# Linear attention on one core: the sine part of the rotated keys written by one VectorE operation instead of two

## The chip, the cores and the metric

One core of one Trainium2 chip runs the program. The metric is the device time of one execution in microseconds. It is given as the median of several runs of the same kernel. The profile is one further execution of it, taken by the hardware profiler.

## What is computed

The program is a chain of layers over x of shape (16, 256, 128): a convolution block, four linear attention layers, a feed-forward layer, and then attention and mixture-of-experts layers. The change lies in the linear attention. Cut to that:

```python
def rope(x):
    ...
    xp = x.reshape(b, n, half, 2)
    xr = jnp.stack([-xp[..., 1], xp[..., 0]], axis=-1).reshape(b, n, c)
    return x * cos + xr * sin

def linear_attention(x, Wq, bq, Wk, bk, Wv, bv, g, bb):
    q = gelu(x @ Wq + bq) + 0.21
    k = gelu(x @ Wk + bk) + 0.21
    v = x @ Wv + bv
    q_r, k_r = rope(q), rope(k)          # then all are split into 16 heads of 8
    z = 1.0 / (jnp.einsum('bhnd,bhmd->bhnm', q, kmean) + 1e-06)
    kv = jnp.einsum('bhnd,bhne->bhde', k_r, v) / n
    out = jnp.einsum('bhnd,bhde->bhne', q_r, kv) * z
    return layernorm(out + x, g, bb)
```

So the channels come in pairs. The rotated key is k*cos plus a sine part, in which each channel takes its partner's value with a sign.

## The kernel before

The program runs its layers as phases. A phase is a block of instruction streams, one for each engine, and a barrier stands between two phases. `linear_phase` holds the four linear attention layers. It works on one batch row of 256 tokens and one layer at a time, and there are 16 x 4 = 64 such units, numbered i. Four rows (U = 4) are in flight, and each has its own buffers and two PSUM banks, A and D. Unit i+4 is the next layer of the same row as unit i (or the first layer of a new row), and it needs what unit i has put out.

The order of work is written out by hand for each engine, in a loop over i from 0 to 66, and semaphores join the engines. In iteration i each engine works on several units:

- **TensorE (PE):** the projections of unit i (L555 for keys and values, L558 for queries); for unit i-1 the sum of the keys (L565), a transpose of the layer's input (L81), and the product of keys and values (L574); for unit i-2 the output (L600, L601); for unit i-3 the transposes back of the normalized rows (L81); then for unit i-1 the turned blocks (L581, which needs L515) and the divisors (L589).
- **VectorE (DVE):** for unit i-3 the statistics of the layer norm (L475, then L482); the bias of keys and values of unit i (L489, which takes what L555 left in PSUM); the reciprocal of unit i-2 (L494); `turn_k` of unit i (L499 for the cosine part into kc, L503 for the sine part into ks); the masked blocks of unit i-1 (L515, reads PSUM and the mask); `join_k` of unit i (L510, adds ks to kc); and the output of unit i-2 (L522, L527).
- **ScalarE (ACT):** gelu of the queries (L634) and of the keys (L639) of unit i; the normalization of unit i-3 (L650); the mean of the keys (L663, L666); the scaled output of unit i-3 (L657), which PE's L555 of unit i+1 needs; then small copies (L644, L671, L676).
- **GpSimd (POOL):** for unit i-3 the reciprocal root and the shift of the layer norm (L448, L449, L451, L454), after L482 and ahead of L650; then for unit i-1 the cosine and sine parts of the queries (L459, L460), each a product of two 256-element tiles in SBUF.

An iteration as it is spoken of here begins with L499 on DVE, so L515, L510, L522, L475, L482, L489 and L494 follow it. `turn_k` waits for gelu of the keys, writes kc in one instruction and ks in two: the first of these fills the even channels from the odd ones, the second the odd from the even. The sine table `sinT` carries the sign. All these tiles are float32 with 128 partitions, and 256 elements on each, 2 halves of 128 channels. No semaphore stands between the three instructions.

Of the kernel before, what the change touches and what calls it, by code (L numbers as in the profile page):

```python
# [12 lines left out]
ALU = mybir.AluOpType  # L13
# [18 lines left out]
GELU_SHIFT = 0.21  # L32
# [19 lines left out]
def semaphores(nc, ctx, prefix, names):  # L52

    sems = {n: nc.alloc_semaphore(f"{prefix}_{n}") for n in names.split()}

    def clear():
        nc.clear_and_free_semaphores(list(sems.values()))
        nc.all_engine_barrier()

    ctx.callback(clear)  # L60
    return sems
# [22 lines left out]
def spread(ap, n):  # L84

    return ap.unsqueeze(len(ap.shape)).broadcast_to([*ap.shape, n])
# [297 lines left out]
def linear_phase(nc, g):  # L384
# [3 lines left out]
    with ExitStack() as ctx:  # L388
        s = semaphores(nc, ctx, "la", "zero pkv pq kv q k qs ks kcs ksum kmean km kvm kvbd kv2 kv2s den dens z qc qsn out yz y "
                                      "stats mv ve nm rstd shift un unt h")  # L390

        def sb(name, shape, dt=F32):
            return ctx.enter_context(nc.sbuf_tensor("la_" + name, shape, dt))
# [5 lines left out]
        h = sb("h", [P, U, N])  # L399
        q = sb("q", [P, U, N])  # L400
        kv = sb("kv", [P, U, NT, 2 * C])
        k = sb("k", [P, U, NT, C])
        kc = sb("kc", [P, U, NT, C])
        ks = sb("ks", [P, U, NT, C])
# [20 lines left out]
        def layer(i):  # L425
            return i // U % L
# [10 lines left out]
        @block.gpsimd  # L437
        def _(pool):
            pool.memset(half[:, :], -0.5).then_inc(s["zero"], 1)
            pool.memset(eps[:, :], LN_EPS_A).then_inc(s["zero"], 1)  # L440
            pool.memset(minus[:, :], -1.0).then_inc(s["zero"], 1)
            pool.memset(ones[:, :], 1.0).then_inc(s["zero"], 1)
            pool.wait_ge(s["zero"], 4)

            def root(i):
                u = i % U
                pool.wait_ge(s["mv"], i + 1)
                pool.tensor_tensor(ve[:, u, :], mv[:, u, :, 1], eps[:, :], ALU.add).then_inc(s["ve"], 1)  # L448
                pool.tensor_tensor(nm[:, u, :], mv[:, u, :, 0], minus[:, :], ALU.mult).then_inc(s["nm"], 1)  # L449
                pool.wait_ge(s["ve"], i + 1)  # L450
                pool.tensor_tensor(rstd[:, u, :], ve[:, u, :], half[:, :], ALU.pow).then_inc(s["rstd"], 1)  # L451
                pool.wait_ge(s["nm"], i + 1)
                pool.wait_ge(s["rstd"], i + 1)
                pool.tensor_tensor(shift[:, u, :], nm[:, u, :], rstd[:, u, :], ALU.mult).then_inc(s["shift"], 1)  # L454

            def turn_q(i):
                u = i % U
                pool.wait_ge(s["qs"], i + 1)
                pool.tensor_tensor(qc[:, u, :], q[:, u, :], g["cosF"][:, :], ALU.mult).then_inc(s["qc"], 1)  # L459
                pool.tensor_tensor(qs[:, u, :], q[:, u, :], g["sinF"][:, :], ALU.mult).then_inc(s["qsn"], 1)  # L460

            for i in range(K + 3):
                if 0 <= i - 3 < K:
                    root(i - 3)
                if 0 <= i - 1 < K:
                    turn_q(i - 1)

        @block.vector
        def _(v):

            def stats(i):
                u = i % U
                v.wait_ge(s["y"], i + 1)
                for t in range(NT):
                    last = v.bn_stats(st[:, u, t, :], y[:, u, t, :])  # L475
                last.then_inc(s["stats"], 1)

            def aggr(i):
                u = i % U
                v.wait_ge(s["stats"], i + 1)  # L480
                for t in range(NT):
                    last = v.bn_aggr(mv[:, u, t, :], st[:, u, t, :])  # L482
                last.then_inc(s["mv"], 1)

            def take_kv(i):
                u = i % U
                bias = g["bkv"][:, layer(i), :].unsqueeze(1).broadcast_to([P, NT, 2 * C])
                v.wait_ge(s["pkv"], i + 1)
                v.tensor_tensor(kv[:, u], A[u].rearrange("p (h c) -> p h c", h=NT), bias, ALU.add).then_inc(s["kv"], 1)  # L489

            def inverse(i):
                u = i % U
                v.wait_ge(s["dens"], i + 1)
                v.reciprocal(z[:, u, :], z[:, u, :]).then_inc(s["z"], 1)  # L494

            def turn_k(i):
                u = i % U
                v.wait_ge(s["k"], i + 1)
                v.scalar_tensor_tensor(out=kc[:, u], in0=k[:, u], scalar=GELU_SHIFT, in1=g["cosT"][:, :, :],  # L499
                                       op0=ALU.add, op1=ALU.mult)  # L500
                for par in range(2):
                    a = [t.rearrange("p h (c t) -> p h c t", t=2) for t in (ks[:, u], k[:, u], g["sinT"][:, :, :])]
                    last = v.scalar_tensor_tensor(out=a[0][:, :, :, par], in0=a[1][:, :, :, 1 - par], scalar=GELU_SHIFT,  # L503
                                                  in1=a[2][:, :, :, par], op0=ALU.add, op1=ALU.mult)
                last.then_inc(s["ks"], 1)

            def join_k(i):
                u = i % U
                v.wait_ge(s["ks"], i + 1)
                v.tensor_tensor(kc[:, u], kc[:, u], ks[:, u], ALU.add).then_inc(s["kcs"], 1)  # L510

            def blocks(i):
                u = i % U
                v.wait_ge(s["kvm"], i + 1)
                v.scalar_tensor_tensor(out=kvbd[:, u, :], in0=A[u][:, 0:C], scalar=1.0 / N, in1=g["head_mask"][:, :],  # L515
                                       op0=ALU.mult, op1=ALU.mult).then_inc(s["kvbd"], 1)

            def scaled(i):
                u = i % U
                v.wait_ge(s["out"], i + 1)  # L520
                v.wait_ge(s["z"], i + 1)
                v.tensor_tensor(y[:, u].rearrange("p h (n d) -> p (h n) d", d=HD),  # L522
                                A[u][:, 0:N].rearrange("p (n d) -> p n d", d=HD),
                                spread(z[:, u, :], HD), ALU.mult).then_inc(s["yz"], 1)
                v.wait_ge(s["yz"], i + 1)
                yu = y[:, u].rearrange("p h c -> p (h c)")
                v.tensor_tensor(yu, D[u][:, 0:N], yu, ALU.add).then_inc(s["y"], 1)  # L527

            for i in range(K + 3):
                if 0 <= i - 3 < K:  # L530
                    stats(i - 3)
                if 0 <= i - 3 < K:
                    aggr(i - 3)
                if 0 <= i - 0 < K:
                    take_kv(i - 0)
                if 0 <= i - 2 < K:
                    inverse(i - 2)
                if 0 <= i - 0 < K:
                    turn_k(i - 0)
                if 0 <= i - 1 < K:  # L540
                    blocks(i - 1)
                if 0 <= i - 0 < K:
                    join_k(i - 0)
                if 0 <= i - 2 < K:
                    scaled(i - 2)
# [2292 lines left out]
```

## Time and profile before

| | us |
|---|---|
| runs of the kernel, median of 3 | 2293.94 |
| lowest and highest of them | 2292.66, 2307.22 |
| span of the profiled execution | 2374.1 |

The profiled execution is slower than the runs, so its durations are read for proportions and order, and a difference in time is set against the span first. In the rows below, times are microseconds from the start of the span unless they are marked ns. PE is TensorE's multiplication, PEld its weight loads, which overlap it. A row names the line of the kernel, the engine, what is written and what is read ("la_ks<-la_k,k_sinT"), the shapes (partitions x elements) and a count. Where neighbouring instructions of one line stand in one row (x2), the time is from the first one's start to the last one's end. "Idle before" and its arrow name what ended the engine's idle time. Instructions of an engine are pipelined, so that one can start slightly before the record of the one ahead ends.

### The profile page before, as it was taken

How to read it: one execution, taken by the hardware profiler on the slowest of the kernel's cores; microseconds unless marked ns; L12 is line 12 of the kernel's file. 1: busy time of each engine (PE TensorE's matmuls, PEld its weight loads, DVE VectorE, ACT ScalarE, POOL GpSimd, SP SyncE). 2: the span in 40 equal slices, each digit the busy share in tenths (PEclk: the TensorE clock that was granted, in tenths of full speed). 3: DMA queues.
4: the chain of work that ended last, by engine and by line, in shares of the span. 5: the costliest groups of instructions: out<-in, count | busy, mean ns of one | idle time of the engine just before them, and what ended most of it. 6: DMA issues, size and time to landing. Idle time of an engine off the chain costs nothing. (4 is left out here: it accounts for less than half of the span.)

```text
span 2374.1 us, 43139 instructions
## 1 busy us (share of the span) xinstructions
PE 1915.4 (81%) x14694; PEld 1329.8 (56%) x14694; DVE 1428.9 (60%) x4140; ACT 1180.8 (50%) x2785; POOL 1135.4 (48%) x2002
## 2 busy tenths in 40 slices
PE   7978999978776888786899888889488887678891
PEld 6866888866332343343455447778234443267781
DVE  6997999955663555475788844323478886333232
ACT  3435666653443677553566544334156764443340
POOL 2534555543354555345567672522666545124225
PEclk9998999999796999898899969899568977589995
DMA  8000000000000000000000005556000000045572
GB/s 259 1 1 1 1 1 1 2 1 0 1 1 1 1 2 1 1 1 1 2 2 2 10 29 154 157 176 194 18 20 6 2 1 24 14 129 176 169 205 78
DMA packets 93945, 109.50 MB, mean 46 GB/s; under 512 B 12945, under 2 KB 76833, under 8 KB 93601
## 3 DMA queue, kind: packets, MB, share of 16 engines
q1 hardware_dynamic: 85536, 89.96, 12.7%
q0 software_dynamic: 8192, 16.79, 2.4%
q8 instruction: 119, 1.95, 0.4%
q14 instruction: 98, 0.80, 0.1%
HBM read 78.14 MB, written 28.57 MB: 45 GB/s over the span
## 5 line engine op out<-in xcount | busy, mean ns | idle before, releaser
L1998 ACT ACTIVATE a2prob<-PS 128x512 f32<-128x512 f32 x256 | 143.9, 598 | 109.5 <-PE PS L1767 82.8
L1535 DVE TENSOR_REDUCE a2mx<-PS 128x4 f32<-128x1024 f32 x128 | 156.0, 1219 | 61.0 <-PE PS L1743 43.1
L2449 POOL DMA_INDIRECT gy<-rows_out,pos x96 | 90.7, 944 | 165.2 <-DMA rows_out<-m1byo 62.7
L1535 DVE TENSOR_REDUCE a1mx<-PS 128x6 f32<-128x768 f32 x128 | 121.8, 952 | 51.4 <-PE PS L1750 50.8
L2001 ACT ACTIVATE a0prob<-PS 128x1024 f32<-128x1024 f32 x128 | 127.3, 1028 | 50.8 <-PE PS L1767 50.5
L1998 ACT ACTIVATE a1prob<-PS 128x384 f32<-128x384 f32 x256 | 116.4, 490 | 72.5 <-PE PS L1767 71.0
L241 DVE SCALAR_TENSOR_TENSOR cv_y<-cv_gl,k_conv_w,cv_y 128x256 f32<-128x256 f32 x320 | 131.3, 477 | 19.6 <-ACT cv_y L349 10.2
L280 PE MATMUL PS<-cv_rT,cv_diag 128*128 128x256 f32 x640 | 142.2, 382 | 0.0
L1360 POOL TENSOR_SCALAR_AFFINE_SELECT a1prob<-a1prob 128x256 f32<-128x256 f32 x256 | 97.8, 411 | 78.7 <-ACT a1prob L1998 78.0
L280 PEld LDWEIGHTS PS<-cv_rT,cv_diag 128*128 128x128 f32 x640 | 121.3, 191 | 16.9
L2480 DVE TENSOR_SCALAR m1ahid<-PS,m1awr 128x256 f32<-128x256 f32 x92 | 40.3, 479 | 148.3 <-PE PS L2577 95.4
L2480 DVE TENSOR_SCALAR m1bhid<-PS,m1bwr 128x256 f32<-128x256 f32 x92 | 40.3, 480 | 146.6 <-PE PS L2577 102.0
L81 PE MATMUL PS<-identb,parts 128*128 128x128 bf16 x1024 | 85.5, 235 | 27.5 <-DVE parts L1550 12.4
L2577 PE MATMUL PS<-m1bxT,m1bwr 128*128 128x256 f32 x368 | 93.5, 399 | 13.9 <-issue 11.4
L2577 PE MATMUL PS<-m1axT,m1awr 128*128 128x256 f32 x368 | 93.6, 400 | 12.0 <-issue 9.3
L2354 POOL DMA_INDIRECT rows_in<-m1an,pos x64 | 62.2, 972 | 73.1 <-DVE pos L2348 44.5
L2588 PE MATMUL PS<-m1awr,m1ahid 128*128 128x128 f32 x736 | 93.3, 282 | 4.3 <-ACT m1ayo L2654 4.3
L81 PEld LDWEIGHTS PS<-identb,parts 128*128 128x128 bf16 x1024 | 68.6, 106 | 47.8 <-issue 36.8
L2354 POOL DMA_INDIRECT rows_in<-m1bn,pos x64 | 61.7, 965 | 69.7 <-DVE pos L2348 41.7
L1743 PE MATMUL PS<-a2kT,a2qT 24*128 24x256 bf16 x512 | 61.8, 327 | 39.9 <-DVE a2mx L1535 33.8
L2588 PEld LDWEIGHTS PS<-m1awr,m1ahid 128*128 128x128 f32 x736 | 89.3, 198 | 4.8 <-ACT m1ayo L2654 4.7
L2588 PE MATMUL PS<-m1bwr,m1bhid 128*128 128x128 f32 x736 | 90.1, 276 | 2.2 <-ACT m1byo L2654 1.6
(528 smaller groups left out, 5402.5 us busy)
## 6 DMA issues: line engine op xcount, KB each, us to landing
m1awr<-in_wtab SPq DMA_DIRECT2D x46, 514.0 KB
m1bwr<-in_wtab SPq DMA_DIRECT2D x46, 514.0 KB
rows_in<-cv_blank SPq DMA_DIRECT2D x46, 128.0 KB, 2.1
m1axin<-rows_in SPq DMA_DIRECT2D x46, 128.0 KB
rows_out<-m1ayo SPq DMA_DIRECT2D x46, 128.0 KB
m1bxin<-rows_in SPq DMA_DIRECT2D x46, 128.0 KB
rows_out<-m1byo SPq DMA_DIRECT2D x46, 128.0 KB
X<-in_x SPq DMA_DIRECT2D x4, 512.0 KB, 6.2
```

Source lines behind the costliest of these rows:

```text
L81: return nc.tensor.matmul(out, lhsT=in_, rhs=ident, start=True, stop=True, is_transpose=True)
L241: v.scalar_tensor_tensor(out=y[:, i % 2, u, :], in0=src, scalar=g["conv2_w"][:, t:t + 1], in1=y[:, i % 2, u, :], op0=ALU.mult, op1=ALU.add)\
L280: last = pe.matmul(bank_c[u][:, j, :], lhsT=diag[:, j * TAPS + k, :], rhs=rT[:, i % 2, u, k:k + N], start=(k == 0), stop=(k == TAPS - 1))
L1360: last = pool.affine_select(out=part, in_=part, compare_op=ALU.is_ge, fill=0.0, base=0, pattern=[[0, NT], [1, P]], channel_multiplier=-1)
L1535: v.tensor_reduce(mx[:, 2 * j:2 * j + 2, :], MB[:, :, 0:SEG * seg_len].rearrange("p h (s n) -> p h s n", n=seg_len), AX.X, ALU.max).then_i ...
L1998: act.activation(prob[:, h % RING, 0:n_prob], SB[(b * NH + h) % NSB][:, 0:n_prob], ACT.Exp, scale=scale).then_inc(s["exp"], 1)
L2001: act.activation(prob[:, h % RING:h % RING + EXPS, :], PS[:, h % NSB:h % NSB + EXPS, :], ACT.Exp, scale=scale).then_inc(s["exp"], EXPS)
L2354: pool.indirect_dma_start(xs[u], bass.IndirectOffsetOnAxis(ap=pos[:, u, k, t:t + 1], axis=0), n[:, u, t, :], None).then_inc(s[f"sc{u}"], 16)
L2449: pool.indirect_dma_start(gy[:, (u * HALF + t) % GY, k, :], None, ys[u], bass.IndirectOffsetOnAxis(ap=pos[:, u, k, t:t + 1], axis=0))\
L2480: last = v.tensor_scalar(hid[:, q % 2, j, :], UP[q % 2][1][:, (j - HJ) * SLOTS:(j - HJ + 1) * SLOTS], wr[:, q % RING, FF + j:FF + j + 1], ...
L2577: last = pe.matmul(UP[q % 2][k][:, j * SLOTS:(j + 1) * SLOTS], lhsT=wr[:, q % RING, at:at + P], rhs=xT[:, q % 2, :], start=True, stop=True)
L2588: last = pe.matmul(DN[:, h * C:(h + 1) * C], lhsT=hid[:, q % 2, j, h * P:(h + 1) * P], rhs=wr[:, q % RING, at:at + C], start=(j == 0), sto ...
```

## The change

The two instructions of the sine part become one. It runs over all 256 elements seen as 128 pairs, and its first input is read with the two elements of each pair in reversed order (a step of -1 within the pair). The output and the table are read and written in plain order. The same semaphore is incremented once, by this instruction. Nothing else of the kernel differs.

```diff
-                for par in range(2):
-                    a = [t.rearrange("p h (c t) -> p h c t", t=2) for t in (ks[:, u], k[:, u], g["sinT"][:, :, :])]
-                    last = v.scalar_tensor_tensor(out=a[0][:, :, :, par], in0=a[1][:, :, :, 1 - par], scalar=GELU_SHIFT,
-                                                  in1=a[2][:, :, :, par], op0=ALU.add, op1=ALU.mult)
-                last.then_inc(s["ks"], 1)
+                pairs = [t.rearrange("p h (c t) -> p (h c) t", t=2) for t in (ks[:, u], k[:, u], g["sinT"][:, :, :])]
+                v.scalar_tensor_tensor(out=pairs[0], in0=pairs[1][:, :, ::-1], scalar=GELU_SHIFT, in1=pairs[2],
+                                       op0=ALU.add, op1=ALU.mult).then_inc(s["ks"], 1)
```

## Rows read from the trace of the kernel before

**Rows 1.** the page, span and section 1: busy us (share) xinstructions
```profile
span 2374.1 us, 43139 instructions
...
PE 1915.4 (81%) x14694; PEld 1329.8 (56%) x14694; DVE 1428.9 (60%) x4140; ACT 1180.8 (50%) x2785; POOL 1135.4 (48%) x2002
```

**Rows 2.** busy time by stretch: start:end length, engines, clock, DMA share, GB/s
```profile
189.00:516.00 327.00, 295.20 (x2048) 265.94 (x2048) 291.26 (x832) 203.28 (x640) 181.89 (x388) 0.99 0.00 1
```

**Rows 3.** who waited for whom, 192 to 508 us: total us, times, longest
```profile
ACT la_un L650 <- POOL la_shift L454: 33.2, 61, 0.5
...
DVE la_kc L499 <- ACT la_k L639: 19.6, 64, 1.0
```

**Rows 4.** timeline of DVE, one iteration: start, us, instruction, idle before
```profile
344.65 0.43 DVE L499 SCALAR_TENSOR_TENSOR la_kc<-la_k,k_cosT 128x256 f32<-128x256 f32 x1 [0.29 <-ACT la_k L639]
344.99 1.02 DVE L503 SCALAR_TENSOR_TENSOR la_ks<-la_k,k_sinT 128x128 f32<-128x128 f32 x2
345.94 0.28 DVE L515 SCALAR_TENSOR_TENSOR la_kvbd<-PS,k_head_mask 128x128 f32<-128x128 f32 x1
346.14 0.74 DVE L510 TENSOR_TENSOR la_kc<-la_kc,la_ks 128x256 f32<-128x256 f32 x1
346.80 0.41 DVE L522 TENSOR_TENSOR la_y<-PS,la_z 128x256 f32<-128x256 f32 x1
...
348.23 0.25 DVE L482 BATCH_NORM_AGGREGATE la_mv<-la_st 128x2 f32<-128x6 f32 x2
348.39 0.66 DVE L489 TENSOR_TENSOR la_kv<-PS,k_bkv 128x512 f32<-128x512 f32 x1
...
349.60 0.42 DVE L499 SCALAR_TENSOR_TENSOR la_kc<-la_k,k_cosT 128x256 f32<-128x256 f32 x1 [0.29 <-ACT la_k L639]
```

**Rows 5.** timeline of POOL, the same iteration
```profile
344.74 0.39 POOL L454 TENSOR_TENSOR la_shift<-la_nm,la_rstd 128x2 f32<-128x2 f32 x1
345.09 0.78 POOL L459 TENSOR_TENSOR la_qc<-la_q,k_cosF 128x256 f32<-128x256 f32 x1
345.83 0.77 POOL L460 TENSOR_TENSOR la_qs<-la_q,k_sinF 128x256 f32<-128x256 f32 x1
...
349.69 0.38 POOL L454 TENSOR_TENSOR la_shift<-la_nm,la_rstd 128x2 f32<-128x2 f32 x1
```

**Rows 6.** timeline of ACT, PE and its loads, the same iteration
```profile
345.16 0.88 ACT L650 ACTIVATE la_un<-la_y,la_shift,la_rstd 128x128 f32<-128x128 f32 x2 [0.55 <-POOL la_shift L454]
...
346.27 0.30 PEld L581 LDWEIGHTS PS<-la_kvbd,k_pair_turn 128*128 128x128 f32 x2
...
346.50 0.52 PEld L589 LDWEIGHTS PS<-la_km,la_q 128*128 128x128 f32 x4
346.57 0.56 ACT L657 ACTIVATE HT<-PS,k_lnA_b,k_lnA_g 128x256 f32<-128x256 f32 x1
...
347.19 0.73 PEld L555 LDWEIGHTS PS<-k_Wkv,HT 128*128 128x128 f32 x4 [0.16 <-ACT HT L657]
...
349.16 0.41 ACT L639 ACTIVATE la_k<-la_kv 128x256 f32<-128x256 f32 x1
```

**Rows 7.** timeline of DVE and POOL, second and third iteration
```profile
197.12 0.72 POOL L459 TENSOR_TENSOR la_qc<-la_q,k_cosF 128x256 f32<-128x256 f32 x1 [2.13 <-ACT la_q L644]
197.30 0.82 DVE L510 TENSOR_TENSOR la_kc<-la_kc,la_ks 128x256 f32<-128x256 f32 x1
...
197.80 0.91 POOL L460 TENSOR_TENSOR la_qs<-la_q,k_sinF 128x256 f32<-128x256 f32 x1
...
202.63 0.41 DVE L510 TENSOR_TENSOR la_kc<-la_kc,la_ks 128x256 f32<-128x256 f32 x1
```

**Rows 8.** three lines in the whole span: ns min/median/max, first and last start
```profile
L499 DVE SCALAR_TENSOR_TENSOR la_kc<-la_k,k_cosT x64: 424/426/426, 193.1 to 503.0; 128x256 f32<-128x256 f32 x64
...
L503 DVE SCALAR_TENSOR_TENSOR la_ks<-la_k,k_sinT x128: 283/288/826, 193.4 to 503.6; 128x128 f32<-128x128 f32 x128
...
L454 POOL TENSOR_TENSOR la_shift<-la_nm,la_rstd x64: 195/383/397, 206.2 to 514.6; 128x2 f32<-128x2 f32 x64
```

## The prediction

> **What bounds it now.** The page comes first: the span is 2374.1 us, DVE is busy for 60% of it and PE for 81% [rows 1]. That says little here, because the changed lines run in one stage only. The busy time by stretch gives that stage 327 us, with DVE busy 291 us and PE 295 us at a granted clock of 0.99, the 2.4 GHz level [rows 2]. An engine busy 89% of a stage looks like its bound. But neither is without gaps: in every iteration DVE waits 0.31 us for ACT's L639, ACT's L650 waits 0.54 for POOL's L454, and PE's load for L555 waits for ACT's L657 [rows 3, 6]. So the iteration must be read in order of time. It repeats every 4.95 us (L499 starts at 344.65 and 349.60) [rows 4]. I count all times from the start S of L499.
>
> What is to be seen in the DVE and POOL rows is that the two block each other where both read SBUF. L499 always takes 426 ns, and L503 has a minimum of 283 ns, but its two instructions here take 1.02 us together [rows 4, 8]: the first ends at S+0.63, and the second ends at S+1.36, just 0.15 after POOL's L459 ended at S+1.22 [rows 4, 5]. L510 takes 0.41 when POOL is still, but 0.82 beside L459, ending 0.28 after it; L460, waiting behind L510, then ends 0.59 after L510 [rows 7]. L515 reads PSUM and keeps its 0.28 while L460 runs [rows 4, 5]. So: a DVE operation with two SBUF inputs held by POOL ends 0.28 (256 elements) or 0.15 (128) after the POOL one; a POOL multiply held by DVE ends 0.59 after the DVE one; and they take turns, the waiting one going before its rival's next.
>
> POOL's small L454 is caught too: minimum 195 ns, median 383 [rows 8]. It starts at S+0.09, sits out L499 and ends at S+0.48. From there L650, the transposes, L657, L555 and L639 lead to the next L499, 4.47 us later [rows 4, 5, 6]. 0.48+4.47 = 4.95: **this loop, L499 holding L454, is the period**, and it contains no L503.
>
> The skill agrees. The Trainium skill (SBUF — State Buffer, "SBUF: two separate sides") says that DVE with two SBUF inputs and a GpSimd operation share a port pair under an exclusive lock kept for the whole instruction. The rows above show the same thing by themselves.
>
> **The change.** Two L503 of 128 elements become one of 256; nothing is moved, no wait or DMA is added, and the one semaphore increment stays. *Own cost.* The nearest rows are two L503 at 0.20 apart from start to start plus the last one's end, about 0.48, against one instruction of L499's form, 0.42 [rows 8]: 0.06 less. *Reversed reading* stands in no row. Below, the bound is nothing extra: L503 already reads and writes every second element and pays 283 ns for 128 beside 426 for 256, a slope of 1.1 ns an element, so stepping across words is free [rows 8]. Above, the first bound is the fixed cost paid a second time, 2 x 283 - 426 = 140 ns, and the far one every element streamed twice, 256 x 1.1 = 0.28 us. I take 0, since the nearest row steps further and pays nothing.
>
> A rule speaks against this. The Trainium skill (Vector Engine (DVE) Microarchitecture Reference, "Measured stream behaviour on trn2") finds full rate only for runs of two adjacent words, 1.73 ns a column for one source that hops each element, and (under "Performance modes") has not measured a negative step. By it L503 should be slow today; the trace shows that it isn't. Were reversed pairs hops, its sum would be (1.73-1.05) x 256 = 0.17 us more an instruction.
>
> *Order with POOL.* The larger effect. The single operation starts at S+0.34, before L459's start at S+0.44, and keeps the port to S+0.68, so L459 cannot slip between the halves. It ends at S+0.77, L459 at +0.59 = S+1.35, L510 at +0.28 = S+1.63, and L522 follows 0.08 before that end, at S+1.56 instead of S+2.15 [rows 4, 5, 7]. DVE's path to L482's end falls from d = 3.83 to d = 1.56+1.68 = 3.24, 0.59 us less.
>
> What is late next? L454 starts 1.21 after the end of L482 [rows 4, 5]. Call its start against the next L499 the lag: lag = d + 1.21 - T, now 3.83+1.21-4.95 = +0.09. The period T is the longest of: (a) L454's end + 4.47; (b) d + 1.05, by L489's end at d+0.57, 0.04, L639's 0.41 and 0.03 [rows 4, 6]; (c) L515's end + 0.04 + 0.67 + 2.41, because PE must load the blocks for L581, then L589, before L555, and L555 precedes the next L499 by 2.41 [rows 4, 6]. The 0.67 is 346.50-346.27 and four loads 0.11 apart; with the idle time as printed it would be 0.76. Now (a), (b), (c) are 4.95, 4.88 and 4.70.
>
> With the change, iteration by iteration:
> - A. Lag +0.09 to +0.16: L454 is still held, T = 4.95, d = 3.24. The next lag is 3.24+1.21-4.95 = -0.50.
> - B. Lag -0.50: L454 is free, but L459 now starts at -0.35 and takes the port before L499. L459 ends at 0.37, L499 at 0.65, L460 at 1.24, the merged operation at 1.52. L515 ends at 1.72, so (c) gives 4.84; L522 is at 1.98, d = 3.66, and (b) gives 4.71. T = 4.84. Next lag: 3.66+1.21-4.84 = +0.03.
> - C. Lag +0.03: L454 ends before it is held, L459 starts at 0.18 and waits out L499. L459 ends at 0.43+0.59 = 1.02, the merged one at 1.30, L460 at 1.89, L510 at 2.17, L522 at 2.09; d = 3.77 and (b) gives T = 4.82. Next lag +0.16, which is A again.
>
> The mean is (4.95+4.84+4.82)/3 = 4.87, 0.08 less than 4.95. Over some 60 steady iterations of 64 [rows 8] that is 4.8 us. If C falls out as A, the two alternate at 4.90 and give 3 us. **The sum against the profile is 2374.1 - 4.8 = 2369.3 us.** The runs' median is 2293.94, 3.4% under that profile; the stage ran at nearly full clock in it, so I carry the difference over unscaled: 2293.94 - 4.8 = **2289 us**. What hides the 0.59 is L499's hold on L454 in A, and POOL's multiplies that hold L499 in B. Without that cover it is rival 2.
>
> **Rivals.**
> 1. *POOL gets ahead for good: slower.* In B, T = lag + 5.34 and d = lag + 4.16, so the next lag is +0.03 whatever it was. It is self-holding if that lag lets L459 (0.15 behind L454) ask before L499. From the rows, L503 beat an L459 that started 0.10 later, so the tip lies near lag -0.10. Some 0.13 us more on (c) gets there; the 0.76 reading gives 0.09 of it. Then T = 5.37, 60 x 0.42 = 25 us: 2319. For it: two of three terms near the edge. Against: the rows put the lag on the safe side.
> 2. *The path falls through.* If neither L454 nor L499 is held, (a) spans two iterations: 2T = d + 1.21 + 0.20 + 4.47 with d = 3.24, plus nothing for the lag, so T = 4.56, 60 x 0.39 = 23 us: 2271. Against: in each turn above one of them is held.
> 3. *Reversed reading costs.* An extra e appears in the port's turns of A, B and C: T rises by e on average. With 0.14, 60 x (0.14-0.08) = +4 us: 2298; with 0.28, +12: 2306.
> 4. *Nothing moves.* The lag stays near +0.09 because some step I take as fixed stretches; (a) gives 4.95 and 2294.
>
> **Chances.** Forecast, mixed turns, 2286 to 2293: 0.48. Rival 4, 2293 to 2297: 0.16. Rival 3: 0.15, of which 0.02 beyond 1%. Rival 1: 0.13, of which 0.09 beyond 1%. Rival 2: 0.08, of which 0.03 beyond 1%. About 1% is what a measurement of this kernel can tell from no change, 23 us. Faster 0.03, same 0.86, slower 0.11. The range leaves out rival 1's far end and the last of rival 2: 2276 to 2307.
>
> **What the profile of the changed kernel would show.** Right: L503 x64 with a minimum near 425 ns, not near 570 or 700; L454 no longer always near 383 ns, with 195 in some iterations; L499 held above 426 in about a third of them; starts of L499 spaced unevenly, near 4.95, 4.84 and 4.82. L503 at 425 in some and near 0.9 us in others. Rival 1 shows L499 long in every iteration and the stage near 352 us; rival 2 shows every spacing near 4.56; rival 4 shows 4.95 throughout. I am wrong if the turns at the port do not follow the order of starts, or if PE's (c) is longer than read.

## The result and the profile after

The changed kernel takes 2291.95 us (median of 20 runs) against 2300.05 for the kernel before (20 runs): a ratio of 0.9969, with a 95% interval of 0.9955 to 0.9982. Measured once more beside the last experiment, it came to 0.9989 (0.9970 to 1.0007), 2297.44 against 2300.30.

In the changed kernel the sine part is L502, the masked blocks L513, the addition L508, the statistics' end still L482, and the gelu of the keys L637; L499, L454, L459 and L460 keep their numbers. First the page, and who waited for whom from 192 to 500 us (total us, times, longest).

```profile
span 2286.5 us, 43075 instructions
...
PE 1868.4 (82%) x14694; PEld 1307.3 (57%) x14694; DVE 1408.6 (62%) x4076; ACT 1184.6 (52%) x2785; POOL 1138.9 (50%) x2002
```

```profile
PEld PS L579 <- DVE la_kvbd L513: 22.3, 31, 1.5
DVE la_kc L499 <- ACT la_k L637: 19.0, 63, 0.7
ACT la_un L648 <- POOL la_shift L454: 16.9, 31, 0.5
```

DVE has 64 instructions less. ACT now waits for L454 31 times instead of 61 [rows 3], and in 31 others PE waits for the masked blocks, which it did not do in the steady part before. So there are two kinds of iteration. The same three lines as in [rows 8], in ns min/median/max, say it too:

```profile
L499 DVE SCALAR_TENSOR_TENSOR la_kc<-la_k,k_cosT x64: 424/426/660, 191.4 to 498.2; 128x256 f32<-128x256 f32 x64
```

```profile
L502 DVE SCALAR_TENSOR_TENSOR la_ks<-la_k,k_sinT x64: 415/420/955, 191.8 to 498.6; 128x256 f32<-128x256 f32 x64
```

```profile
L454 POOL TENSOR_TENSOR la_shift<-la_nm,la_rstd x64: 195/198/472, 203.9 to 509.2; 128x2 f32<-128x2 f32 x64
```

L499 is now held in some iterations, L454 is free in half of them, and the merged operation takes 0.42 or 0.95. Two iterations in order of time, DVE first, POOL below:

```profile
341.21 0.43 DVE L499 SCALAR_TENSOR_TENSOR la_kc<-la_k,k_cosT 128x256 f32<-128x256 f32 x1 [0.29 <-ACT la_k L637]
341.55 0.42 DVE L502 SCALAR_TENSOR_TENSOR la_ks<-la_k,k_sinT 128x256 f32<-128x256 f32 x1
341.89 0.28 DVE L513 SCALAR_TENSOR_TENSOR la_kvbd<-PS,k_head_mask 128x128 f32<-128x128 f32 x1
342.09 0.75 DVE L508 TENSOR_TENSOR la_kc<-la_kc,la_ks 128x256 f32<-128x256 f32 x1
342.76 0.41 DVE L520 TENSOR_TENSOR la_y<-PS,la_z 128x256 f32<-128x256 f32 x1
...
344.19 0.25 DVE L482 BATCH_NORM_AGGREGATE la_mv<-la_st 128x2 f32<-128x6 f32 x2
...
346.16 0.65 DVE L499 SCALAR_TENSOR_TENSOR la_kc<-la_k,k_cosT 128x256 f32<-128x256 f32 x1 [0.29 <-ACT la_k L637]
346.74 0.95 DVE L502 SCALAR_TENSOR_TENSOR la_ks<-la_k,k_sinT 128x256 f32<-128x256 f32 x1
347.61 0.28 DVE L513 SCALAR_TENSOR_TENSOR la_kvbd<-PS,k_head_mask 128x128 f32<-128x128 f32 x1
347.81 0.41 DVE L508 TENSOR_TENSOR la_kc<-la_kc,la_ks 128x256 f32<-128x256 f32 x1
...
351.02 0.43 DVE L499 SCALAR_TENSOR_TENSOR la_kc<-la_k,k_cosT 128x256 f32<-128x256 f32 x1 [0.29 <-ACT la_k L637]
```

```profile
341.23 0.47 POOL L454 TENSOR_TENSOR la_shift<-la_nm,la_rstd 128x2 f32<-128x2 f32 x1
341.65 0.91 POOL L459 TENSOR_TENSOR la_qc<-la_q,k_cosF 128x256 f32<-128x256 f32 x1
342.52 0.91 POOL L460 TENSOR_TENSOR la_qs<-la_q,k_sinF 128x256 f32<-128x256 f32 x1
...
345.66 0.20 POOL L454 TENSOR_TENSOR la_shift<-la_nm,la_rstd 128x2 f32<-128x2 f32 x1
345.81 0.73 POOL L459 TENSOR_TENSOR la_qc<-la_q,k_cosF 128x256 f32<-128x256 f32 x1
346.50 0.91 POOL L460 TENSOR_TENSOR la_qs<-la_q,k_sinF 128x256 f32<-128x256 f32 x1
...
351.04 0.47 POOL L454 TENSOR_TENSOR la_shift<-la_nm,la_rstd 128x2 f32<-128x2 f32 x1
```

The first iteration, 341.21 to 346.16, lasts 4.95 us: L499 holds L454 to 341.70, which is 0.49 after S (0.48 before) [rows 4, 5], and the merged operation runs ahead of L459. DVE's path to the end of L482 has fallen from 3.83 to 344.44-341.21 = 3.23. So L454 starts 0.50 ahead of the next L499, and L459 takes the port before it. In the second, 346.16 to 351.02, 4.86 us, L499 and the merged operation are both held, and the masked blocks end only at 347.89. PE's loads then set the end of it:

```profile
347.94 0.30 PEld L579 LDWEIGHTS PS<-la_kvbd,k_pair_turn 128*128 128x128 f32 x2 [0.69 <-DVE la_kvbd L513]
...
348.61 0.73 PEld L553 LDWEIGHTS PS<-k_Wkv,HT 128*128 128x128 f32 x4
```

From the fifth L499 to the last, the starts lie 4.906 us apart on average, against 4.949 before. The stage, from its first projections to its last instruction, takes 323.7 us, against 327.2 (from its first memset on, 324.3 against 327.8). Of these 3.5 us the steady iterations give 59 x 0.043 = 2.5. Most of the rest lies between the first and the fifth L499, 17.4 us here and 18.0 before. That part can't be put down to the change: it is 16.6 us in halves, which has the period of before, and 15.9 in forward, which has the period of the changed kernel.

### The profile page after: what moved, and what is told of

Same layout as the page of the kernel before. It is cut to its first block and busy times, and to the rows that moved or that the text cites. A ratio compares the mean times of both kernels' runs of the same rounds, so it can differ in the third digit from the quotient of the medians.

```text
span 2286.5 us, 43075 instructions
## 1 busy us (share of the span) xinstructions
PE 1868.4 (82%) x14694; PEld 1307.3 (57%) x14694; DVE 1408.6 (62%) x4076; ACT 1184.6 (52%) x2785; POOL 1138.9 (50%) x2002
## 5 line engine op out<-in xcount | busy, mean ns | idle before, releaser
L81 PE MATMUL PS<-identb,parts 128*128 128x128 bf16 x1024 | 83.0, 231 | 28.5 <-DVE parts L1548 12.9
L81 PEld LDWEIGHTS PS<-identb,parts 128*128 128x128 bf16 x1024 | 66.4, 104 | 47.4 <-issue 35.7
L2575 PE MATMUL PS<-m1axT,m1awr 128*128 128x256 f32 x368 | 88.2, 383 | 2.7 <-ACT m1axT L2637 2.7
```

Source lines behind the costliest of these rows:

```text
L81: return nc.tensor.matmul(out, lhsT=in_, rhs=ident, start=True, stop=True, is_transpose=True)
L2575: last = pe.matmul(UP[q % 2][k][:, j * SLOTS:(j + 1) * SLOTS], lhsT=wr[:, q % RING, at:at + P], rhs=xT[:, q % 2, :], start=True, stop=True)
```

## The experiments

Each ratio is to the kernel before, measured beside it on the same chip, with its 95% interval. Its median was 2300.05 us beside the changed kernel, 2299.38 beside the next four of the table, 2299.49 beside forward, short_root, best and tiny_q, and 2300.30 beside changed_again. The ratio is not the quotient of the two medians, and differs from it by up to 0.4% (halves). "Spacing" is the mean distance between the starts of the cosine operation from the fifth to the last in the profile. "Stage" and spacing come from one profiled execution each. What each kernel is, is told below the table. Line numbers shift by a few from kernel to kernel.

| kernel | spacing, us | stage, us | median, us | ratio |
|---|---|---|---|---|
| before | 4.949 | 327.2 | 2300.05 | 1 |
| changed | 4.906 | 323.7 | 2291.95 | 0.9969 (0.9955 to 0.9982) |
| late_q_two | 4.423 | 293.3 | 2268.00 | 0.9855 (0.9819 to 0.9890) |
| late_q_one | 4.392 | 291.1 | 2274.61 | 0.9887 (0.9857 to 0.9917) |
| halves | 4.947 | 326.7 | 2309.16 | 1.0004 (0.9970 to 1.0038) |
| early_blocks | 4.793 | 315.0 | 2296.28 | 0.9977 (0.9955 to 0.9999) |
| forward | 4.906 | 322.2 | 2297.30 | 0.9994 (0.9975 to 1.0013) |
| short_root | 5.015 | 329.2 | 2296.49 | 0.9993 (0.9974 to 1.0012) |
| best | 4.392 | 290.0 | 2256.55 | 0.9819 (0.9790 to 0.9847) |
| tiny_q (one run) | 4.394 | 293.7 | 2262.52 | |
| changed_again | 4.906 | 324.2 | 2297.44 | 0.9989 (0.9970 to 1.0007) |

**Does the shared port set the period?** The kernel before, with POOL's multiplies moved out of the way of the three DVE operations with two SBUF inputs:

```diff
                 pool.wait_ge(s["qs"], i + 1)
+                pool.wait_ge(s["kcs"], min(i + 2, K))
                 pool.tensor_tensor(qc[:, u, :], q[:, u, :], g["cosF"][:, :], ALU.mult).then_inc(s["qc"], 1)
```

> The kernel before (two sine operations), with one wait added on POOL, so that its two multiplies for the queries start only after DVE's addition of ks to kc. They then lie beside DVE operations that read PSUM or one SBUF tile. Theory (turns at the shared port set the period): neither engine holds the other, the addition takes 0.41 us, the path to the statistics' end falls from 3.83 to about 2.98, the small POOL operation before the normalization is free (195 ns), and the period is (2.98+1.21+0.20+4.47)/2 = 4.43 instead of 4.95: 60 x 0.52 = 31 us faster. Rival (DVE is simply full, 89% busy; the long durations are those of the operations themselves): the durations stay and the period stays at 4.95, no change.

It came out so: 4.423 for 4.43, and a ratio of 0.9855, 33 us less. POOL does the same work and has one more wait. The loop over two iterations closes in the trace: DVE's path takes 2.97 (340.29 to 343.26), then 1.22 to the start of L454, 0.20 for it and 4.46 to the start of L500 two iterations on, 8.85 together, or 4.43 each.

```profile
340.29 0.43 DVE L500 SCALAR_TENSOR_TENSOR la_kc<-la_k,k_cosT 128x256 f32<-128x256 f32 x1 [0.29 <-ACT la_k L640]
...
343.01 0.25 DVE L483 BATCH_NORM_AGGREGATE la_mv<-la_st 128x2 f32<-128x6 f32 x2
...
344.48 0.20 POOL L454 TENSOR_TENSOR la_shift<-la_nm,la_rstd 128x2 f32<-128x2 f32 x1
...
349.14 0.43 DVE L500 SCALAR_TENSOR_TENSOR la_kc<-la_k,k_cosT 128x256 f32<-128x256 f32 x1 [0.29 <-ACT la_k L640]
```

The two sine operations and the addition (lines 504 and 511 of that kernel) show durations without the long ones of before:

```profile
L504 DVE SCALAR_TENSOR_TENSOR la_ks<-la_k,k_sinT x128: 283/286/295, 201.1 to 478.0; 128x128 f32<-128x128 f32 x128
```

```profile
L511 DVE TENSOR_TENSOR la_kc<-la_kc,la_ks x64: 406/416/424, 201.6 to 478.4; 128x256 f32<-128x256 f32 x64
```

Was it the wait that did something else? Here no wait is added, and the multiplies are cut to two elements in the changed kernel (that their outputs are set to 0 once at the start is left out here):

```diff
-                pool.tensor_tensor(qc[:, u, :], q[:, u, :], g["cosF"][:, :], ALU.mult).then_inc(s["qc"], 1)
-                pool.tensor_tensor(qs[:, u, :], q[:, u, :], g["sinF"][:, :], ALU.mult).then_inc(s["qsn"], 1)
+                pool.tensor_tensor(qc[:, u, 0:2], q[:, u, 0:2], g["cosF"][:, 0:2], ALU.mult).then_inc(s["qc"], 1)
+                pool.tensor_tensor(qs[:, u, 0:2], q[:, u, 0:2], g["sinF"][:, 0:2], ALU.mult).then_inc(s["qsn"], 1)
```

> The changed kernel with POOL's two multiplies for the queries cut from 256 to 2 elements, the rest of their outputs left at zero; no wait is added. Theory (the multiplies' hold on the port is what sets the period): the period falls to 4.39, as when the multiplies are merely moved, and no DVE operation is held. Rival (the wait that was added did something else, as shifting PE's work): the period stays near 4.9.

The spacing is 4.394, against 4.392 in the changed kernel with the wait (late_q_one, next): taking the multiplies away gives what moving them gives. The rival falls. Both stand where PE takes over (see the last of these experiments), so this shows that the multiplies held the period at 4.9, not how far it could fall without them.

**What is the change worth with the port free?** The changed kernel with the same wait on POOL:

> The changed kernel with the same wait on POOL. Theory: the port is free, so the merged operation saves only its own 0.06 us on a loop that spans two iterations: a period of 4.40, 0.03 less than with two operations, 2 us less in all, where the change gave 0.04 an iteration with the port contended. About 33 us faster than the kernel before. Rival (the change is worth its saved DVE time however the port is shared): 4 us or more less than the same kernel with two operations.

The spacing fell by 0.031, from 4.423 to 4.392, as the loop over two iterations has it; with the port contended the change gave 0.043. The runs don't resolve this: late_q_one came out slower than late_q_two by 0.3%, within the two intervals, though its stage is 2.2 us shorter. Against the kernel before it is 26 us less where 33 were expected, at the edge of its interval. But 4.392 is not only that loop, see the last experiment.

**Is it the count or the reading?** Two operations as before, split by token half, each reading its pairs in reversed order:

```diff
-                for par in range(2):
-                    ...
-                    last = v.scalar_tensor_tensor(out=a[0][:, :, :, par], in0=a[1][:, :, :, 1 - par], ...
+                pairs = [t.rearrange("p h (c t) -> p h c t", t=2) for t in ...]
+                for part in range(NT):
+                    last = v.scalar_tensor_tensor(out=pairs[0][:, part], in0=pairs[1][:, part, :, ::-1], ...
```

> The kernel before with its two sine operations split by token half instead of by parity, each reading its pairs in reversed order. Theory (what counts is that POOL can get in between two operations): reversed reading is free, each takes 283 ns where not held, and the period is that of before, 4.95 in every iteration; time equal to before within 1 us. Rival (the gain is from reading and writing adjacent words, not from the count): a minimum below 283 ns and a time nearer to that of the changed kernel, 8 us less than before.

```profile
L503 DVE SCALAR_TENSOR_TENSOR la_ks<-la_k,k_sinT x128: 283/285/822, 198.2 to 506.9; 128x128 f32<-128x128 f32 x128
```

The minimum is 283 ns and the maximum 822, as with every second element (283 and 826) [rows 8], and the spacing is 4.947. Adjacent words gain nothing and reversed ones cost nothing; with two operations POOL gets in between. This rests on the profile: the runs can't show equality within 1 us. Their ratio is 1.0004 (0.9970 to 1.0038), but the median is 2309.16 against 2299.38, because 7 of the 12 runs took 2308 to 2319 us and 5 took 2284 to 2299. Why is not known.

The merged operation with plain instead of reversed reading:

```diff
-                v.scalar_tensor_tensor(out=pairs[0], in0=pairs[1][:, :, ::-1], scalar=GELU_SHIFT, in1=pairs[2],
+                v.scalar_tensor_tensor(out=pairs[0], in0=pairs[1], scalar=GELU_SHIFT, in1=pairs[2],
```

> The changed kernel with the pairs read in plain order, so that the sine part takes each channel's own value instead of its partner's. All else is the same. Theory (reversed reading is free): the merged operation has the same minimum, 415 ns, the iterations alternate between 4.95 and 4.86 as in the changed kernel, and the time is the changed kernel's, about 7 us less than before. Rival (a reversed pair costs something): a minimum below 415 ns and a shorter time than the changed kernel's.

```profile
L502 DVE SCALAR_TENSOR_TENSOR la_ks<-la_k,k_sinT x64: 415/421/955, 191.7 to 497.0; 128x256 f32<-128x256 f32 x64
```

The durations are those of the reversed one, 415/420/955, and so is the spacing. The time was not: 1.4 us less than before (0.9994), where 7 were expected. Two programs with the same spacing thus differed by 0.25% against their own controls, though their intervals overlap. So the changed kernel was measured again:

> The changed kernel itself, measured once more. Its stage is 3.5 us shorter than that of the kernel before by the profiles, while its time was measured 7 us less and that of the same kernel with plain reading, whose stage is as short, 1 us less. Theory (the stage is all that differs, the rest is scatter between programs and chips): a ratio near 0.9985, that is 3 to 4 us less. Rival (the change gains something outside the stage, or in executions that are not profiled): a ratio near 0.997 again.

0.9989, 2.5 us less. The 3.5 us of the stage (0.9985) and the 2.5 of its steady iterations (0.9989) lie within this interval and that of forward, and outside the first one's upper end of 0.9982. The three together don't ask for a gain outside the stage. What scatters between them is not shown.

**What sets the second kind of iteration?** DVE's masked blocks ahead of the cosine and sine operations, and PE's product ahead of its sum so that they are ready:

```diff
 # VectorE
+                if 0 <= i - 1 < K:
+                    blocks(i - 1)
                 if 0 <= i - 0 < K:
                     turn_k(i - 0)
-                if 0 <= i - 1 < K:
-                    blocks(i - 1)
 # TensorE
+                if 0 <= i - 1 < K:
+                    keys_values(i - 1)
                 if 0 <= i - 1 < K:
                     sum_k(i - 1)
-                if 0 <= i - 1 < K:
-                    keys_values(i - 1)
```

> The changed kernel, with PE's product of keys and values ahead of its sum of keys, and DVE's masked blocks ahead of the cosine and sine operations. It takes the masked blocks away from behind the held operation, and nothing else. Theory (iterations alternate: one of 4.95 in which the cosine operation holds the small POOL operation, one of 4.86 that is set by the masked blocks coming late to PE): the first stays at 4.95, the second falls to 4.51, then set by DVE's path to the gelu of the keys; mean 4.73, 60 x 0.22 = 13 us less than the kernel before, 10 less than the changed one. Rival (the iteration of 4.86 is set by DVE's own length): no change against the changed kernel.

The starts alternate between 4.95 and 4.64. The first kind is untouched and the second fell, so the blocks did set it. PE's order was changed with DVE's and was not run alone, but the wait is seen to go: from 250 to 450 us PE waited for the masked blocks 20 times in the changed kernel and never here. The second kind fell by 0.22 instead of 0.35. These rows of DVE show why:

```profile
345.62 0.64 DVE L499 SCALAR_TENSOR_TENSOR la_kc<-la_k,k_cosT 128x256 f32<-128x256 f32 x1
346.18 0.95 DVE L502 SCALAR_TENSOR_TENSOR la_ks<-la_k,k_sinT 128x256 f32<-128x256 f32 x1
347.17 0.42 DVE L508 TENSOR_TENSOR la_kc<-la_kc,la_ks 128x256 f32<-128x256 f32 x1
```

L508 waits for what the operation directly ahead of it writes, and starts 0.04 after its end (347.13), where an instruction that doesn't wait starts 0.08 before the end. The masked blocks had covered that. With d = 349.19-345.62 = 3.57 the path to the gelu gives 3.57+1.05 = 4.62, and 4.63 was seen here. The runs gave 0.9977, 5 us less, with 9 expected of the spacing, inside the interval.

**Can less work on POOL be slower?** This tests the slow rival's mechanism, that POOL gets ahead for good (that the mean `nm` is set to 0 once at the start is left out here):

```diff
-                pool.tensor_tensor(ve[:, u, :], mv[:, u, :, 1], eps[:, :], ALU.add).then_inc(s["ve"], 1)
-                pool.tensor_tensor(nm[:, u, :], mv[:, u, :, 0], minus[:, :], ALU.mult).then_inc(s["nm"], 1)
-                pool.wait_ge(s["ve"], i + 1)
-                pool.tensor_tensor(rstd[:, u, :], ve[:, u, :], half[:, :], ALU.pow).then_inc(s["rstd"], 1)
-                pool.wait_ge(s["nm"], i + 1)
+                pool.tensor_tensor(rstd[:, u, :], mv[:, u, :, 1], half[:, :], ALU.pow).then_inc(s["rstd"], 1)
```

> The changed kernel with less work on POOL ahead of the normalization: the addition of epsilon and the negated mean are left out (the mean taken as 0), 0.30 us less between the statistics' end and the small operation that computes the shift. Theory (turns at the port): the small operation now starts 0.91 after the statistics instead of 1.21, early enough that POOL's first multiply always takes the port ahead of DVE's cosine operation. The lag settles at 4.17+0.91-5.37 = -0.29, the cosine operation takes about 0.65 us in every iteration and the period is 5.08 in all of them: 60 x 0.17 = 10 us slower than the changed kernel though less is done. Rival (POOL's chain is work on the path, so less of it is faster): period at or below 4.91, time equal to the changed kernel's or up to 9 us less.

POOL's first multiply (L456 there) now leads the cosine operation (L496) in every iteration, and both the cosine and the sine operation (L499) are held:

```profile
344.32 0.73 POOL L456 TENSOR_TENSOR la_qc<-la_q,k_cosF 128x256 f32<-128x256 f32 x1
344.52 0.81 DVE L496 SCALAR_TENSOR_TENSOR la_kc<-la_k,k_cosT 128x256 f32<-128x256 f32 x1 [0.29 <-ACT la_k L634]
345.00 0.92 POOL L457 TENSOR_TENSOR la_qs<-la_q,k_sinF 128x256 f32<-128x256 f32 x1
345.25 0.95 DVE L499 SCALAR_TENSOR_TENSOR la_ks<-la_k,k_sinT 128x256 f32<-128x256 f32 x1
```

Every steady iteration lasts 5.00 to 5.03 us. That is 0.11 more than in the changed kernel (0.17 expected). The small operation starts 0.35 ahead of L496 (0.29 expected), L496 takes 0.81 instead of 0.65, and the period is 5.02 instead of 5.08. The stage is 5.5 us longer, with less work in it. The total, 0.9993, does not resolve this against the changed kernel (0.9969 and 0.9989). By the profile, then, the self-holding order exists, and the changed kernel is not in it.

**A faster kernel, and the next bound.** The wait on POOL, the early blocks and no addition of epsilon together:

> The changed kernel with three edits: POOL's two multiplies wait for the addition of ks to kc; PE's product of keys and values and DVE's masked blocks are early; the addition of epsilon (1e-12) on POOL is left out. Theory: with the port free the period is half of the loop over two iterations, (2.81+1.06+0.20+4.47)/2 = 4.27, 0.12 less than with the first edit alone: 60 x 0.68 = 41 us less than the kernel before. Rival (PE, busy 89%, is now the bound): the period stays near the 4.39 of the first edit alone.

It is the fastest, 2256.55 us or 0.9819, 42 us less than the kernel before. That this meets the expected 41 is luck: the spacing is 4.392, that of late_q_one, not 4.27, and it gives 59 x 0.557 = 33 us. The busy time from 250 to 450 us says what holds it: PE is busy for 196 of 200 us, at a granted clock of 1.00, where the changed kernel has 183. It is 197 in late_q_two, late_q_one and tiny_q.

```profile
250.00:450.00 200.00, 196.37 (x1456) 184.75 (x1456) 175.79 (x548) 138.45 (x456) 112.45 (x230) 1.00 0.01 1
```

One handover to ACT stands in PE's way, the scaled output (L654 here), in every iteration:

```profile
341.41 0.38 PE L81 MATMUL PS<-k_ident,la_un 128*128 128x128 f32 x2
341.83 0.56 ACT L654 ACTIVATE HT<-PS,k_lnA_b,k_lnA_g 128x256 f32<-128x256 f32 x1 [0.21 <-PE PS L81]
342.44 0.73 PEld L552 LDWEIGHTS PS<-k_Wkv,HT 128*128 128x128 f32 x4 [0.17 <-ACT HT L654]
```

From PE's load for L552 (338.05) to the end of L81 (341.79) PE works without a wait for 3.74 us, and L654 with its handovers takes 0.65 to the next load for L552 at 342.44, in which PE's other work covers all but about 0.07. Together they are the 4.39. So for the period the rival was right: PE is the bound at 4.39, with this one handover. That late_q_one has just this spacing means that its agreement with 4.40 is half an accident: the loop and PE give the same number there. The stage of best is only 1.1 us shorter than that of late_q_one, so most of the 18 us between their medians is not explained by the stage; the spread between programs seen above may hold part of it.

## Why the prediction was right, point by point

- *The bound.* Right, and shown: the period came from L499 holding L454 and from turns at the port, not from DVE's or PE's load. Moving the multiplies took 11% off the period at the same work.
- *The merged operation's cost.* Expected about 0.42 with reversed reading free; measured 415 to 420 ns where not held, the same as with plain reading. Rival 3 fell.
- *The order with POOL.* Right: d fell from 3.83 to 3.23 (3.24 expected), the lag went to -0.50, and L499 was held to 0.65 in the second kind.
- *Iteration B.* 4.86 measured, 4.84 worked out, by the term that was named, (c): 347.89+0.05+0.67+2.41 = 351.02.
- *Iteration C.* Here the step failed. The lag after B was +0.01 (351.04-351.02), +0.03 expected, but L454 was held at that lag all the same, to 0.49 after S. I had let it pass ahead of L499, though it starts after it. The traces fit a port that goes to whoever starts first, down to hundredths. At lags of 0.00 to +0.02 the small operation was held in all seven profiles that have such lags (0.46 to 0.47 us). The one time that it started 0.02 ahead of the cosine operation, early in best (L452 and L498 there), it took 0.20, and the cosine operation 0.45 instead of 0.43:

```profile
204.05 0.20 POOL L452 TENSOR_TENSOR la_shift<-la_nm,la_rstd 128x2 f32<-128x2 f32 x1
204.07 0.45 DVE L498 SCALAR_TENSOR_TENSOR la_kc<-la_k,k_cosT 128x256 f32<-128x256 f32 x1
```

  So C falls out as A, and the two alternate at a mean of 4.906, the second way that the prediction gave (4.90). The saving of the stage is 3.5 us by the profiles, 2.5 of it in the steady iterations (3 by that way), not 4.8.
- *The time.* 2289 was predicted from the earlier median of 2293.94; the measured 2291.95 stands against 2300.05. The measured gain is 8 us by the medians, 7 by the ratio, and 2.5 in the second measurement, against 4.8 predicted. That the time came within 3 us of 2289 is partly luck: the base was 6 us higher than the one that was counted from, and the first measured gain was 3 us larger than forecast, while the stage is only 3.5 and 3.0 us shorter in the two profiles of the changed kernel. The runs can't tell a change of 3 us well; the mechanism rests on the profiles.
- *Rival 1.* The self-holding order was real, but needed the shorter POOL chain of short_root; it cost 0.11 an iteration over the changed kernel there. *Rival 2* did not happen, though 4.42 with the port free is less than the 4.56 that it gave. *Rival 4* is ruled out by the spacings.

## What to carry to other kernels

A busy share of 89% did not make an engine the bound; the sum of small holds in one loop did, and they show as a duration far above the same line's minimum. Where DVE operations with two SBUF inputs and POOL operations meet, first put POOL's work beside DVE operations that read PSUM or one SBUF tile: one wait gave 33 us here, where one instruction less gave about 3. When a path is shortened inside such a loop, work out who comes first at the port in the next iteration, since the gain can be taken back there.

## What was not expected of the hardware

- The order at the port can settle into patterns of its own: one iteration long (before, 4.95; short_root, 5.02) or two (4.95 and 4.86 in turn), from nearly the same work with other offsets.
- POOL's operation on 2 elements took 195 ns or, started 0.01 us after L499, 467 ns; it was held even when it started practically together with it, and not the one time when it started 0.02 ahead.
- Reading a float32 pair in reversed order cost nothing (415 ns against 415), nor did reading and writing every second element (283 ns for 128 elements against 283 reversed).
- An operation of DVE that waits for the one directly ahead started 0.04 us after its end instead of 0.08 before it (L508 in early_blocks).
